# Whole groups of P times V or two projections between the score bursts of a fused attention layer

## The reference

```python
x_seq = x.reshape(B, S, d_model)                      # 16, 900, 512
q, k, v = proj(wq, bq), proj(wk, bk), proj(wv, bv)    # each 16, 8, 900, 64
scores = einsum('bhqd,bhkd->bhqk', q, k) / sqrt(64) + bias_matrix
attn = softmax(scores, axis=-1)
ctx = einsum('bhqk,bhkd->bhqd', attn, v).reshape(B, S, d_model)
resid = ctx @ wo + bo + x_seq
out = (resid - mean) * rsqrt(var + 1e-5) * gamma + beta
```

## Time and profile before

| | |
|---|---|
| median of three runs | 3212.4 us (3210.62 to 3213.43) |
| the profiled execution | 3212.19 us, its span 3210.2 us |
| PE busy | 3098.7 us, 97% |
| ACT busy | 2713.9 us, 85% |
| DVE busy | 2610.0 us, 81% |
| POOL busy | 1603.4 us, 50% |
| mean granted TensorE clock | 0.993 |

### The profile page before, as it was taken

The page is one execution under the profiler, slowest core; times in us unless marked ns, Lnnn a source line. Parts: engine busy times, 40 slices in busy tenths (PEclk is TensorE's granted clock), DMA queues, the critical chain, the costliest instruction groups (busy, mean ns, idle before and its releaser), DMA issues. The chain is left out here.

```text
span 3210.2 us, 126640 instructions
## 1 busy us (share of the span) xinstructions
PE 3098.7 (97%) x52264; PEld 2079.8 (65%) x52264; DVE 2610.0 (81%) x5594; ACT 2713.9 (85%) x6903; POOL 1603.4 (50%) x3277
## 2 busy tenths in 40 slices
PE   8899999999999999999999999999999999999986
PEld 5566666666666666666666666666666666666655
DVE  3878879798797978879788797977969788797887
ACT  4988888888888888898888988888888988888885
POOL 1346445465554645546454454645536455464544
PEclk9999999999999999999999999999999999999998
DMA  7332423324233342423324233242332424333231
GB/s 199 73 84 73 94 70 91 77 73 105 62 92 87 76 96 65 96 80 82 85 76 92 71 89 82 73 97 67 95 86 70 98 66 91 86 75 92 65 79 28
DMA packets 523289, 267.80 MB, mean 83 GB/s; under 512 B 329274, under 2 KB 460346, under 8 KB 522590
## 3 DMA queue, kind: packets, MB, share of 16 engines
q1 hardware_dynamic: 375479, 127.82, 18.2%
q10 hardware_dynamic: 147232, 131.88, 14.0%
HBM read 194.10 MB, written 63.44 MB: 80 GB/s over the span
## 5 line engine op out<-in xcount | busy, mean ns | idle before, releaser
L1000 DVE CUSTOM_DVE_ANT_0 prob<-s_ps,window 128x450 f32<-128x450 f32 x1920 | 1107.9, 613 | 441.4 <-PE s_ps L720 441.3
L842 ACT ACTIVATE prob<-prob,own 128x450 f32<-128x450 f32 x1920 | 1265.4, 662 | 142.7 <-DVE own L1000 129.3
L858 ACT ACTIVATE prob<-prob,weight 128x450 f32<-128x450 f32 x1920 | 1173.5, 660 | 47.0 <-POOL weight L1147 44.1
L1016 DVE STREAM_TRANSPOSE prob_t<-prob 128x960 f32<-128x960 f32 x960 | 1125.8, 1173 | 72.7 <-PE pv_ps L740 39.9
L740 PEld LDWEIGHTS pv_ps<-prob_t,values 64*64 64x64 f32 x30720 | 753.6, 133 | 378.0 <-issue 330.9
L720 PE MATMUL s_ps<-k_sb,q_sb 64*32 64x450 f32 x15360 | 853.2, 546 | 38.1 <-DVE own L1000 34.3
L740 PE MATMUL pv_ps<-prob_t,values 64*64 64x120 f32 x30720 | 857.8, 260 | 24.4 <-ACT ctx_sb L868 21.5
L634 PE MATMUL r_ps<-xt,w_sb 128*128 128x450 f32 x3072 | 704.1, 376 | 8.8 <-ACT prob_t L816 3.7
L634 PEld LDWEIGHTS r_ps<-xt,w_sb 128*128 128x128 f32 x3072 | 564.4, 190 | 92.5 <-issue 27.2
L1133 POOL TENSOR_TENSOR lead<-own,other 128x4 f32<-128x4 f32 x480 | 102.1, 213 | 985.0 <-DMA other<-own 984.7
L1147 POOL TENSOR_TENSOR weight<-total,minus_one 128x4 f32<-128x4 f32 x480 | 502.8, 1048 | 37.7
(11 more groups left out here) (63 smaller groups left out, 1488.0 us busy)
## 6 DMA issues: line engine op xcount, KB each, us to landing
w_sb<-w_split ACTq DMA_DIRECT2D x126, 512.0 KB, 4.0
values<-v_dram ACTq DMA_DIRECT2D x256, 240.0 KB, 3.2
other<-own SPq DMA_DIRECT2D x1920, 1.0 KB, 2.2
tokens<-in_x SPq DMA_DIRECT2D x420, 64.0 KB, 3.1
tokens<-in_x SPq DMA_DIRECT2D x109, 240.0 KB, 3.1
out<-tokens SPq DMA_DIRECT2D x105, 240.0 KB, 2.7
v_dram<-stage SPq DMA_DIRECT2D x90, 240.0 KB, 2.8
v_dram<-stage SPq DMA_DIRECT2D x30, 180.0 KB, 2.3
```

Of the source, the lines that this page charges most:

```text
L842: nc.scalar.activation(prob[:, im.unit(u) % RING, head, 0:HALF], prob[:, im.unit(u) % RING, head, 0:HALF], ACT.Exp, scale=-1.0, bias=own[: ...
L858: nc.scalar.activation(prob[:, im.unit(u) % RING, head, 0:HALF], prob[:, im.unit(u) % RING, head, 0:HALF], ACT.Copy, scale=weight[:, s, c: ...
L1000: nc.vector.tensor_tensor_reduce(prob[:, im.unit(u) % RING, head, 0:HALF], s_ps[:, u % 2, head, 0:HALF], window[:, w0:w0 + HALF // GRID, : ...
L1016: nc.vector.transpose(out=prob_t[:, g % 2, v % PER_GROUP, :, :].rearrange("p h k -> p (h k)"), in_=prob[:, im.unit(u) % RING, :, :].rearra ...
```

## The change

Between two bursts of scores there is now as a rule either one whole group of P times V or two whole projections. A table GAPS names the projections of each slot; 18 slots have some. Slots 0, 16, 28 and 46 hold a whole group and one projection, slots 4, 8, 12, 20, 24, 30, 34, 38, 42, 50, 54 and 58 a whole group alone, the other 14 two projections alone. Groups 7 and 15 are done two units sooner. With it go other bodies for the evictions, the context splits, the loads and the splits of x; the store of a value tile stands ahead of the exchange in SP's body and one body sooner; turn_x runs one body ahead of the split and not two. The waits in keep_context and split_context are written differently and have the same values.

```diff
-PV_UNITS = [4, 8, 12, 16, 20, 24, 28, 32, 34, 38, 42, 46, 50, 54, 58, 62]
-PV_CUT = 8
-SPLIT_UNITS = [0, 0, 4, 6, 8, 11, 14, 17]
-LOAD_X = [22, 24, 28, 32]
+PV_UNITS = [4, 8, 12, 16, 20, 24, 28, 30, 34, 38, 42, 46, 50, 54, 58, 60]
+SPLIT_UNITS = [0, 0, 3, 4, 8, 9, 12, 15]
+LOAD_X = [19, 22, 26, 30]
+X_UNITS = [30, 31, 33, 34, 37, 38, 41, 42]
...
-def pv_parts(u, last=False):
...
+def pv_groups(u, last=False):
+    return [g for g, at in enumerate(PV_UNITS) if (min(at, UNITS) if last else at) == u]
...
-def place(items):
...
-STEPS, EVICT = place(SEQUENCE)
+GAPS = {0: pieces(1, (3,)), 2: [out(0), out(1)], 6: [out(2), out(3)], 10: [out(4)] + pieces(2, (0,)),
+        14: [out(5)] + pieces(2, (1,)), 16: pieces(2, (2,)), 18: [out(6)] + pieces(2, (3,)), 22: [out(7)] + pieces(3, (0,)),
+        26: pieces(3, (1, 2)), 28: pieces(3, (3,)), 32: [value(0), value(1)], 36: [value(2), value(3)],
+        40: [value(4), value(5)], 44: [value(6)] + pieces(4, (0,)), 46: pieces(4, (1,)), 48: pieces(4, (2, 3)),
+        52: [value(7)] + pieces(5, (0,)), 56: pieces(5, (1, 2))}
+SEQUENCE = [item for u in sorted(GAPS) for item in GAPS[u]]
+EVICT = {item: u + (2 if n and item[0] != "out" else 1) for u in GAPS for n, item in enumerate(GAPS[u])}
...
-X_UNITS = [u - 1 for u in VALUE_UNITS[:NT - 1]]
-X_UNITS += [X_UNITS[-1] + 1]
...
             def body(im, u):                                   # SP
+                for work in im.evicted(u):
+                    if work[0] == "value":
+                        keep_value(im, work[1])
                 if u % 2 and im.live(u + 5):
                     exchange(im, u + 5)
...
-                for work in im.evicted(u - 1):
-                    if work[0] == "value":
-                        keep_value(im, work[1])
...
-                for of, g, j0, j1 in im.parts(u):              # PE
-                    context(of, g, j0, j1)
+                for of, g in im.groups(u):
+                    context(of, g)
                 for work in im.background(u):
-                    work_on(im, work[:-2], *work[-2:])
+                    work_on(im, work)
...
                 for t in range(X_TILES):                       # VectorE
-                    if X_UNITS[t] - 2 == u and not im.last:
+                    if X_UNITS[t] - 1 == u and not im.last:
                         turn_x(im, t)
```

More of the change, by code:

```diff
@@ L144, in background @@
 def background(u, first, last):
-    work = [(*item, k0, k1) for item, k0, k1 in STEPS.get(u, []) if wanted(item, first, last)]
+    work = [item for item in GAPS.get(u, []) if wanted(item, first, last)]
     if last:
-        work += [("final", t, 0, KT) for t in range(NT) if FINAL_UNITS[t] == u]
+        work += [("final", t) for t in range(NT) if FINAL_UNITS[t] == u]
     return work
 def order(first, last):
-    return [w[:-2] for u in range(END) for w in background(u, first, last) if w[-1] == steps(w)]
+    return [w for u in range(END) for w in background(u, first, last)]
 def evicted(u, first, last):
@@ L205, in live, with groups @@
         return not (self.first and u < 0) and not (self.last and u >= UNITS)
-    def parts(self, u):
-        before = [] if self.first else [(Before(self), *part) for part in pv_parts(u + UNITS)]
-        return before + [(self, *part) for part in pv_parts(u, self.last) if u < UNITS or self.last]
+    def groups(self, u):
+        before = [] if self.first else [(Before(self), g) for g in pv_groups(u + UNITS)]
+        return before + [(self, g) for g in pv_groups(u, self.last) if u < UNITS or self.last]
     def background(self, u):
@@ L619, in piece @@
                 bank, pair = bank_of(use), im.pair(p)
[L620 to L632, removed]
+                bank_wait(im, use)
+                if im is pro and j == 0:
+                    first_xt_ready(NT - 2)
+                    first_xt_ready(NT - 1)
+                if j == 0 and p == PAIRS and im is not pro:
+                    pe.wait_ge(x_lo, X_TILES * (im.b + 1))
+                if half == 0:
+                    if known(pair):
+                        pe.wait_ge(lo_done[("wk0", "wq0")[kind]], 1)
+                    else:
+                        pe.wait_ge(w_in[kind], 16 * pair)
+                for k in range(KT):
                     for i, (a, c) in enumerate(TERMS):
@@ L643, in value_tile @@
                 at = HALF * half + j
[L644 to L650, removed]
+                bank_wait(im, ("value", t))
+                if im is not pro:
+                    pe.wait_ge(x_lo, X_TILES * im.b + x_tiles_to(at + n))
+                elif t == 0:
+                    pe.wait_ge(lo_done["wv"], 1)
+                for k in range(KT):
                     for i, (a, c) in enumerate(TERMS):
@@ L694, in work_on @@
                 else:
[L695 removed]
+                    out_tile(im, work)
             def scores(im, u):
@@ L722, in scores, with context @@
                 last.then_inc(scores_full, 1)
-            def context(im, g, j0, j1):
+            def context(im, g):
                 p, gi = divmod(g, PAIR_GROUPS)
                 n, group = group_units(g), im.group(g)
[L729 to L735, removed]
+                pe.wait_ge(turned, im.unit(PER_PAIR * p + PER_GROUP * gi + n))
+                if gi == 0:
+                    pe.wait_ge(v_in[p % 2], 64 * (PAIRS // 2 * im.b + p // 2 + 1))
+                if not known(group):
+                    pe.wait_ge(ctx_kept, group)
+                for j in range(BLOCKS):
                     for a in range(2):
@@ L914, in body @@
                         stage_value(im, work[1])
-                for of, g, j0, j1 in im.parts(u - 1):
-                    if j1 == BLOCKS:
-                        keep_context(of, g)
+                for of, g in im.groups(u - 1):
+                    keep_context(of, g)
                 if im.live(u + AHEAD):
```

80 lines of the change are left out of this document (23 added, 57 removed).

## The result

The changed kernel takes 3245.5 us (median, 3241.1 to 3247.8), the one before 3212.6 on the same chip: ratio 1.010, 95% interval 1.008 to 1.012. It is slower by 33 us; forecast were 47 us less. The profiled execution has a span of 3243.8 us.

The account below looks back on a forecast made before the run. PE was taken to bound most slots, with DVE level in slots 2 to 24. 3212.2 us less 54 (3.6 a middle image) gave 3158; 7 for clock falls made it 3165, range 3145 to 3178 (chance 0.48).

Parts of the forecast that it names:

- What bounds: Whole kernel: PE sets the pace of most slots; in slots 2 to 24 PE and DVE are level.
- the cost of a burst: On PE: 0.175 us a burst of projections, 0.16 a cut group; together 4.3 us an image taken from PE.
- B: Slots 26 to 58 and slot 0 of the next image: bound by PE alone, from 115.8 to 112.2 us.
- A: Slots 2 to 24: the saving runs into DVE, so 79.7 us before and after.
- rival 3: On PE: burst costs don't go but sit in the scores' neighbours; 3212 us, chance 0.06.
- rival 5: Slots 2 to 24: DVE doesn't bind, so the saving comes through there too; 3129 us, chance 0.07.
- what the change asks of SP: Bodies 30, 33 and 34: more loads and stores ahead of exchanges, costed at nothing, at most 2 us an image.
- the wait for the split x goes: Value tiles in B: x tiles split earlier, so PE's wait of 1.0 us an image goes.
- The bookkeeping: Slots 2 to 24: following PE's starts and DVE's reads gave waits of 0.4 (slot 6), 2.8 (slot 10), 0.9 us (slot 14).
- The clock: Slot 10: one fall to half speed in every fifth image, 2.5 us each, 7 us in all.
- Rival 2: Slots 6 to 10 and 14: PE starves, the clock falls behind both, 5.9 us an image; 3244 us, chance 0.12.
- rival 4: In B: SP's crowd makes ACT late by 2 us an image; 3186 us, chance 0.12.

Follow-up runs that it names:

- e4: The changed kernel with VectorE's centring and normalisation of output tiles on 64 of 512 columns, the rest left out: 3180.3 us, ratio 0.990.
- f4: The changed kernel with GpSimd's add of the bias to the residual on 64 of 512 columns, the rest left out: 3214.5 us, ratio 1.000.
- e3: The changed kernel with the lone pieces of slots 0, 16, 28 and 46 fetched by ScalarE one body later: 3198.5 us, ratio 0.997.
- e1: The changed kernel with the load of x tile 3 in SP's body 28 instead of 30: 3208.3 us, ratio 0.999.
- g3: The changed kernel with e1, e3, x tile 7 loaded in body 35, odd-body splits ahead of lead, GpSimd's bias add one body later: 3133.1 us, ratio 0.974.
- g2: The changed kernel with e1, e3, x tile 7 loaded in body 35, and GpSimd's bias add one body later: 3147.8 us, ratio 0.979.

## Why the prediction was wrong

**What bounds, and the cost of a burst: right.** PE bounds B, and VectorE and PE bound A (e4 and f4: the time of A follows VectorE). Built up from 1.67, 3.24, 2.49 and 0.175 for a burst, sixteen of B's eighteen slots come within 0.1 us. That speaks against rival 3, and e4 and f4 against rival 5.

**Stretch B: the step that failed.** It is the sentence on what the change asks of SP: "while ACT has 192 - 168.5 = 23 us of slack an image; I cost it at nothing", with 2 us as the other bound. The measured size is 5.0 us an image (117.19 against 112.2), 4.4 of it in slot 40: 3.1 of waiting for the split x, and the rest with the falls of the clock there. Three things were wrong in it. First, I followed the late exchange to ScalarE's ratio alone. It is GpSimd that waits for it, in lead, and the split of x for the value tiles is queued behind; PE waits for that. I named what stands behind the waiting instruction for one consumer and not for the other. Second, slack over an image is no slack in a stretch of it: SP issued for 29 us without a pause (1544.95 to 1573.89). Third, I took the evictions as they stood. That the lone pieces of four slots are fetched before they are done can be read from GAPS and EVICT alone; e3 gives 47 us for it, the most of the single edits to B. The claim that the wait for the split x goes was the reverse of what came: 49.0 us instead of 15.7. With these mended (e1, e3, the load of tile 7, and the split ahead of lead) B is 112.10 (g3), the forecast's 112.2: what it said of PE alone holds when nothing else is late.

**Stretch A: the mechanism right, a term too small.** The bookkeeping of starts against VectorE's reads put waits in slots 6 and 10, and there they are, if longer: slots 8 and 10 lose 5.2 us together against 2.8 forecast. The bookkeeping took 0.9 us for a normalisation from the earlier trace rows, and two in a body beside two adds of GpSimd take 1.38 each. That is 1.0 us a pair, on a path where VectorE is 6 us behind; and the longer wait brings the clock down. f4 and g2 show it: without the meeting A is 79.02 and 78.33, under the 79.7 forecast. That it comes out under says that 0.9 was no price of a normalisation alone either. In the kernel before 37 of the 120 overlap an add of GpSimd and take 1.16 us in the mean, the other 83 take 0.75; in the changed kernel 66 overlap one, at 1.38, and 54 take 0.79; in g2 and g3 none does, at 0.73. So 0.9 mixed two prices, and the sum of A came near by two misses of opposite sign. That two output tiles side by side in one slot would bring two of GpSimd's adds beside two of VectorE's normalisations was to be seen in the table of bodies. The Trainium skill has the rule for it: by "SBUF — State Buffer", section "SBUF: two separate sides", a VectorE operation with two operands in SBUF and a GpSimd operation that reads SBUF exclude each other for the whole instruction. The trace agrees in the main: the normalisation reads tokens and beta_all, and went from 0.69 to 1.38 us each; the add went from 1.28 to 1.50. It doesn't agree to the letter: one after the other the two pairs would take 1.37 + 2.56 = 3.93 us, and from the first start (1461.68) to the last end (1465.22) they took 3.54.

**The clock: counted too low.** One fall in five images was put in; in images 1 to 14 there are 22, 12 at slot 10 and 10 at slot 40, each time during or behind the waits there (in image 7 those of 2.18 and 3.12 us). The forecast had 7 us for the clock; by PE's busy time it was some 40. That is 1.8 a fall where 3.4 had been put (2.5 after what comes back), so the price was high and the count far too low. A wait there didn't always bring a fall: in image 10 PE waited 3.07 us in slot 40, in image 9 2.19 and 1.17 us in slot 10, and the clock held. The rule of the Trainium skill, page "TensorE: Matmul & The Clock Gate", section "Why this matters for your kernels", by which only longer gaps matter, would have had no fall behind slot 10, whose single waits were 2.45 us at most; this trace doesn't bear it out.

**The rivals.** Rival 2 gives 3244, and 3245 came, but that is luck, since only half of its story did: slots 6 to 10 starve and the clock falls behind them, which is 1.5 us an image more in A than the forecast, not 5.9. The rest is rival 4, SP's crowd, at two and a half times its price (5.0 us an image against 2) and through another engine. Its bound of 2 us had been worked out from ScalarE's ratio. The two together had 0.24 of the chance and were held to be alternatives; they came together, and the clock falls behind the waits of both.

**What stays open.** In slot 32 PE stops amid the scores with nothing but issue as the reason (0.49 us in the rows above), while loads of x and weights are under way; 0.4 us are left in g3 (7.82 against 7.40 of slot 36, which does the same). Its cause is open; nothing was tried on it. That waits bring the clock down was seen, not varied on its own, and why waits of the same length sometimes didn't is open. How much of A's gain in g2 is the shorter normalisation and how much the clock, which falls in 9 places fewer, isn't separated.

## What to carry to other kernels

Before an edit that makes slots uneven, draw up a table of bodies: for each engine's queue (DMA issues with 0.6 to 0.9 us each among them) what comes in which body, what it waits for, and what is queued behind it; slack over an image covered nothing in a burst of seven bodies here. Let every consumer fetch in the body in which its producer is done, not one sooner. And put large GpSimd and VectorE operations on SBUF operands into different bodies: here one body's shift of an add was worth 1.4% of the time.

## What the runs showed of the hardware

- VectorE's normalisation of 120x512, with two operands in SBUF, took 0.69 us alone (g3, mean of all 0.73) and 1.38 beside GpSimd's add of the same shape, which itself went from 1.28 to 1.50.
- In images 1 to 14 of the changed kernel, with PE busy 96%, the clock fell to 1.2 GHz 22 times, at the slots with waits of 2 to 4 us (slot 10: two waits close together, of some 2.2 and 1 us); beside 60 us of further waits it cost some 40 us, two thirds as much again. One wait of 3.07 us brought no fall.
- SP took 0.6 to 0.9 us to issue a DMA, so the four of an exchange took 2.5 to 3.5 us and four loads of x 2.7 to 3.3.
